# A fused attention and feed-forward kernel: the first output tiles prepared and projected inside the last attention group

## The chip, the cores and the metric

The kernel runs on one core of a Trainium2 chip. The metric is the device time of one execution in microseconds (us), the median of several runs. The engines are TensorE (PE; its weight loads are listed as PEld), VectorE (DVE), ScalarE (ACT), GpSimd (POOL) and SyncE (SP), which here only issues DMAs. Each engine works through its own program in order; they are tied together by semaphores.

## The reference

One layer on an input of 2 x 1024 x 512 in float32: attention with 32 heads of 16 numbers (queries and keys clipped and normalised, a linear position bias, a causal mask), an output projection, a residual, and then a normalised product with a weight summed from four sign matrices, with a residual again.

```python
    x = L0_attn_hidden_states
    x = x + _L0_attn_ref(_layernorm(x, axis=-1), L0_attn_Wqkv, ..., L0_attn_Wout)
    x = x + _L0_ffn_ref(_layernorm(x, axis=-1), L0_ffn_bases, L0_ffn_alphas)
    return x
```
Inside the attention `probs = softmax(scores)`, `out = einsum('bhqk,bkhd->bqhd', probs, v)` and the result is `einsum('bsd,ed->bse', out, Wout)`. Inside the second part `W_q = sum(alphas * bases, axis=0)` and the result is `einsum('bsi,oi->bso', x, W_q)`.

## The kernel before

The kernel has three stages in one program. Stage one projects 16 tiles of 128 tokens to queries, keys and values and stores them in device memory. Stage two is the attention. Stage three takes the 16 tiles again: the **output stage**.

**Attention.** There are 16 groups (0 to 15) of four heads; groups 0 to 7 are the first batch row, which is output tiles 0 to 7. A group has 12 units (a block of 128 keys against up to 512 queries), and the units are cut into 40 **entries** (`NE`), each one exponential on ACT (`probs<-ps`, L781). A step `s` of the loop `exp_step` is entry `s % 40` of group `s // 40`; the last group, 15, is steps 600 to 639, and its entries are called e0 to e39 below. At every step each engine emits what belongs to it. PE computes the scores of the entry in one of four rotating PSUM banks (L1098: a first product, and a second that is added to it; even entries use the lower 64 rows of the array and odd ones the upper 64), and six steps behind it multiplies a whole unit of exponentials with the values (L1133, called **weighing**). POOL masks the diagonal entries (L673), which are e0 to e11 and e28 to e39. Since there are four score banks, PE is at most four entries ahead of ACT. The running maxima of a group (PE L1078, DVE L951) are computed one group ahead, so that they are over before group 15 begins and DVE has nothing to do in it but the inversion below. When half a group is weighed, ACT copies it to `o_sb` (L809, `copy_half`) and SP stores it (L506). In group 15 the first copy comes at e18 and the second after e39.

**Output stage.** For each tile t, SP loads the attention output `o_in` and the reciprocal sums `inv_in` (L529, L532) and the residual `x2` (L536). POOL multiplies them (`att`, L687), ACT rounds the product to the short format (`att_hi`, L803), POOL takes the rest (`att_lo`, L691), and PE multiplies both with the output weight: 12 matmuls of 128x512, four each of L1012, L1013 and L1014, into PSUM bank 0 or 1. DVE adds the residual (L973), takes the statistics (L976, L978), ACT the square root (`y_sd`, L822), DVE the reciprocal and the normalised tile `yn` (L982, L986). PE transposes it (L1020, four matmuls), ACT and DVE split it into `yt_hi` and `yt_lo` (L829, L992), PE multiplies with the second weight (again 12 matmuls), DVE adds the residual (`y_out`, L1001) and SP stores the tile. The loop is staggered: in its step s PE does the projection of tile s+2, the transposes of s+1 and the second product of s.

**Weights.** Each of the two weights of this stage is kept as a rounded part and a rest. The rest `wffn_lo` of the second weight is made by POOL (`low_chunk`, L596, four chunks) after all steps of the attention. The tiles of the output stage share memory with the unrounded weights, so SP may load nothing into them before both weights are done (`wout_ready`, `wffn_ready`).

**Sums.** The sums of the exponentials of a batch row lie in device memory beside the attention output. SP loads them (`sums`, L542), DVE inverts them (`invert`, L956), SP stores the reciprocals (`inv_dram`, L547) and then loads them per tile in the wide form. For the first batch row this is done around group 15, for the second in the output stage.

The order on each engine is fixed by the program text: there is no scheduler. The parts of SP's program that matter are the function `group_step(s)` for s = 14 and 15, of which the second runs after SP has stored the halves of the groups before.

## Time and profile before

| | |
|---|---|
| runs | 725.4, 720.21, 721.72 us |
| median | 721.72 us |
| profiled execution | 724.78 us |
| its span in the profile | 723.0 us |
| busy: PE, DVE, ACT, POOL | 678.8, 575.2, 411.4, 312.9 us |
| mean granted TensorE clock | 0.962 |
| attention's last weighing ends | 609.84 us |
| last instruction (`y_out` of tile 15) starts | 719.82 us |

All times in the rows are microseconds from the start of the span. The 1.8 us between the span and the time of the profiled execution lie around the program.

### The profile page before, as it was taken

The page shows a single profiled execution, that of the slowest core. Times are in us where ns is not written, and L with a number is a line of the kernel's source. Part 1 is how long each engine was busy: PE and PEld are TensorE (multiplying, and loading weights), DVE is VectorE, ACT ScalarE, POOL GpSimd, SP SyncE. Part 2 cuts the span into 40 slices and gives each one's busy share as a digit, 9 for nine tenths or more (in the row PEclk, how much of TensorE's full clock was granted, in tenths as well). Part 3 has the DMA queues.
Part 4 walks back from the last instruction along what each step waited for, and adds up shares of the span by engine and source line. Part 5 has one row for each costly group of instructions (what it writes and reads, how often), then busy time and mean ns, then how long its engine had stood idle before and what let it go on. Part 6 is the DMA issues. An engine that isn't in the chain of part 4 may idle for free.

```text
span 723.0 us, 16007 instructions
## 1 busy us (share of the span) xinstructions
PE 678.8 (94%) x6096; PEld 416.4 (58%) x6096; DVE 575.2 (80%) x990; ACT 411.4 (57%) x855; POOL 312.9 (43%) x403
## 2 busy tenths in 40 slices
PE   3999999997999999999999999999899896599998
PEld 2888888883354454444455455444445532488886
DVE  6799999988999889998998899799899810275664
ACT  5132333232078778887787788678778886222221
POOL 1377777777034625525426422322332234444440
PEclk9999999997579999999999999999999999699999
DMA  8225556777884342343344334324434111635441
GB/s 297 65 68 174 175 175 194 199 201 215 264 183 106 117 127 86 98 125 116 90 123 122 91 108 125 110 78 125 114 94 117 50 35 23 170 103 156 145 148 66
DMA packets 102060, 93.64 MB, mean 130 GB/s; under 512 B 11640, under 2 KB 81912, under 8 KB 101984
## 3 DMA queue, kind: packets, MB, share of 16 engines
q1 hardware_dynamic: 97856, 86.84, 41.4%
q10 hardware_dynamic: 2016, 3.67, 1.7%
q0 software_dynamic: 2112, 2.10, 1.5%
q8 instruction: 49, 0.80, 0.5%
q14 instruction: 27, 0.22, 0.1%
HBM read 57.44 MB, written 33.82 MB: 126 GB/s over the span
## 4 chain that ended last, share of the span: by engine, by line
PE 71%; DVE 15%; issue 8%; POOL 3%; ACT 2%; DMA 1%; SPq 0%; DVEq 0%; POOLq 0%; ACTq 0%
PE ps L1098 23%; PE ps L1133 20%; PE ps L1078 9%; PE ps L1012 5%; PE ps L1013 5%; PE ps L1014 5%; DVE stats L951 3%; DVE qk_stat L896 2%; DVE qk L892 2%; PE ps L1020 2%; PE ps L1074 2%; DVE x_stat L862 1%; DVE xt_lo L855 1%; DVE rest L871 1%; DVE v_ext L905 1%
## 5 line engine op out<-in xcount | busy, mean ns | idle before, releaser
L951 DVE TENSOR_REDUCE stats<-ps 128x1 f32<-128x512 f32 (+3 forms) x608 | 359.4, 656 | 43.9 <-PE ps L1078 42.2
L781 ACT ACTIVATE probs<-ps 128x512 f32<-128x512 f32 (+2 forms) x640 | 310.2, 560 | 83.4 <-PE ps L1098 82.9
L1078 PE MATMUL ps<-first_k,first_q 54*128 54x128 bf16 (+3 forms) x1152 | 219.9, 284 | 5.6 <-DVE stats L951 5.2
L1098 PE MATMUL ps<-second_q,second_k 64*128 64x128 bf16 (+4 forms) x1152 | 206.2, 276 | 0.0
L1098 PE MATMUL ps<-first_q,first_k 54*128 54x512 bf16 (+3 forms) x768 | 197.0, 331 | 9.3 <-issue 9.2
L673 POOL TENSOR_SCALAR_AFFINE_SELECT probs<-probs 128x256 f32<-128x256 f32 x256 | 102.5, 406 | 144.2 <-ACT probs L781 136.9
L1133 PE MATMUL ps<-probs,v_sb 128*32 128x512 f32 (+3 forms) x1536 | 157.9, 498 | 1.8 <-issue 0.8
L1098 PEld LDWEIGHTS ps<-first_q,first_k 54*128 54x128 bf16 x768 | 58.2, 95 | 121.8 <-ACT probs L781 108.1
L1078 PEld LDWEIGHTS ps<-first_k,first_q 54*128 54x128 bf16 x1152 | 92.7, 96 | 49.3 <-DVE stats L951 34.7
L1098 PEld LDWEIGHTS ps<-second_q,second_k 50*128 50x128 bf16 (+1 forms) x1152 | 92.9, 96 | 21.4 <-issue 2.1
L1012 PE MATMUL ps<-wqkv_hi,xt_hi 128*128 128x512 f32 x192 | 77.3, 403 | 0.0
L1014 PE MATMUL ps<-wqkv_hi,xt_lo 128*128 128x512 f32 x192 | 75.8, 395 | 0.0
L1013 PE MATMUL ps<-wqkv_lo,xt_hi 128*128 128x512 f32 x192 | 75.7, 394 | 0.0
L614 POOL TENSOR_TENSOR qk<-qk,qk_gain 128x1024 f32<-128x1024 f32 x16 | 38.4, 2399 | 59.9 <-DVE qk L913 59.9
L653 POOL TENSOR_TENSOR shift_lo<-shift,shift_hi 32x128 bf16<-32x128 f32 x16 | 6.7, 418 | 131.8 <-ACT shift_hi L765 131.8
L973 DVE TENSOR_TENSOR x<-ps,x 128x512 f32<-128x512 f32 x16 | 11.0, 687 | 58.9 <-PE ps L1014 58.9
L1133 PEld LDWEIGHTS ps<-probs,v_sb 128*32 128x32 f32 x1536 | 33.9, 108 | 34.9 <-ACT probs L781 15.1
L1074 PE MATMUL ps<-mask_sb 64*128 64x256 bf16 x256 | 51.0, 280 | 0.0
L751 ACT ACTIVATE qk_sd<-qk_mv,eps 128x2 f32<-128x2 f32 x16 | 4.7, 296 | 69.6 <-DVE qk_mv L899 69.6
L1014 PEld LDWEIGHTS ps<-wqkv_hi,xt_lo 128*128 128x128 f32 x192 | 36.6, 191 | 8.0
L1012 PEld LDWEIGHTS ps<-wqkv_hi,xt_hi 128*128 128x128 f32 x192 | 36.8, 191 | 7.2
L1013 PEld LDWEIGHTS ps<-wqkv_lo,xt_hi 128*128 128x128 f32 x192 | 36.7, 191 | 7.2
(79 smaller groups left out, 822.1 us busy)
## 6 DMA issues: line engine op xcount, KB each, us to landing
parts_dram<-parts SPq DMA_DIRECT2D x48, 256.0 KB, 4.0
v_dram<-v_ext SPq DMA_DIRECT2D x16, 512.0 KB, 4.0
v_sb<-v_dram SPq DMA_DIRECT2D x16, 512.0 KB, 4.4
o_dram<-o_sb SPq DMA_DIRECT2D x32, 256.0 KB
first_q<-parts_dram SPq DMA_DIRECT2D x96, 64.0 KB
first_k<-parts_dram SPq DMA_DIRECT2D x96, 64.0 KB
second_q<-parts_dram SPq DMA_DIRECT2D x96, 64.0 KB
second_k<-parts_dram SPq DMA_DIRECT2D x96, 64.0 KB
```

Of the source, the lines that this page charges most:

```text
L614: pool.tensor_tensor(qk[t % 2][:], qk[t % 2][:], qk_gain[:], ALU.mult).then_inc(qk_scaled, 1)
L673: pool.affine_select(out=turned, in_=turned, compare_op=ALU.is_ge, fill=0.0, base=0, pattern=[[0, 2], [1, P]], channel_multiplier=-1).then ...
L781: act.activation(weights, scores, ACT.Exp, scale=SCALE).then_inc(exp_done, 1)
L892: dve.tensor_scalar(qk[t % 2][:], ps[:, bank:bank + 2, :], CLIP, -CLIP, ALU.min, ALU.max).then_inc(qk_clipped, 1)
L951: dve.tensor_reduce(to, scores, AX.X, ALU.max).then_inc(max_taken, 1)
L1012: pe.matmul(to, hi[:, c, :], w_hi[:, c, :], start=(c == 0), stop=False)
L1013: pe.matmul(to, hi[:, c, :], w_lo[:, c, :], start=False, stop=False)
L1014: last = pe.matmul(to, lo[:, c, :], w_hi[:, c, :], start=False, stop=(c == DC - 1))
L1074: pe.matmul(ps[:, bank, :].rearrange("p (r h t) -> p r h t", r=G, h=2)[:, :, h, :], late_q[h][mine, :], one_hot[mine, :, :], start=(h == 0 ...
L1078: last = pe.matmul(ps[:, bank, r * cols:(r + 1) * cols], first_q[n % STACKS][rows, hp, i * P:(i + 1) * P], first_k[n % STACKS][rows, hp, k ...
L1098: return pe.matmul(ps[:, bank, r * cols + first:r * cols + last], stack_k[n % STACKS][rows, heads[r] // PAIR, kb * P:(kb + 1) * P], stack_ ...
L1133: last = pe.matmul(ps[j * VW:(j + 1) * VW, PV_BANK, to:to + cols], v_sb[n % 2][:, kb, j * VW:(j + 1) * VW], probs[w % P_SLOTS][:, j, 0:col ...
```

## The change

Four things move from the output stage into groups 14 and 15.

- The four chunks of `wffn_lo` are made on POOL in the steps of group 14 (`LOW_AT`, entries 13, 16, 19 and 22).
- SP waits for both weights at the end of `group_step(14)`, then loads the sums, the three first residuals, stores the reciprocals and loads tiles 0 and 1; after the first `att` it loads tile 2. All of this now stands ahead of the stores of group 14's second half and of both halves of group 15. `load_sums` waits for the first batch row's stores alone.
- POOL multiplies tiles 0, 1 and 2 at e13, e15 and e22 of group 15 (`attend`), and takes the rests of tiles 0 and 1 at e18 and e20 (`low_attention`). ACT rounds them at e17, e19 and e30 (`high_attention`).
- PE projects tiles 0 and 1 in eight pieces of three matmuls, one behind each of the entries e24 to e31 (`PROJ_AT`). Tile 2 is projected after the last weighing, ahead of the transposes of tile 0. PE's wait for the last copy to `o_sb` is dropped.

```diff
+LOW_AT = [(GROUPS - 2) * NE + 13 + 3 * c for c in range(DC)]
+LAST_GROUP = (GROUPS - 1) * NE
+AHEAD = 2
+ATT_AT = [LAST_GROUP + 13, LAST_GROUP + 15, LAST_GROUP + 22]
+ATT_HIGH_AT = [LAST_GROUP + 17, LAST_GROUP + 19, LAST_GROUP + 30]
+ATT_LOW_AT = [LAST_GROUP + 18, LAST_GROUP + 20]
+PROJ_AT = [LAST_GROUP + 24 + c for c in range(AHEAD * DC)]
...
                 if s == GROUPS - 2:
-                    load_sums(0)
-                if s == GROUPS - 1:
-                    store_inverses(0)
-
-                    sp.wait_ge(inv_stored, 16)
+
                     sp.wait_ge(wout_ready, DC)
                     sp.wait_ge(wffn_ready, DC)
+                    load_sums(0)
                     for t in range(3):
-                        if t == 2:
-                            sp.wait_ge(att_ready, 1)
+                        load_residual(t)
+                    store_inverses(0)
+                    sp.wait_ge(inv_stored, 16)
+                    for t in range(AHEAD):
                         load_sums_of_tile(t)
-                        load_residual(t)
+                    sp.wait_ge(att_ready, 1)
+                    load_sums_of_tile(AHEAD)
...
-                    sp.wait_ge(o_stored[half], 16 * (GROUPS if b else GROUPS - 1 - half))
+                    sp.wait_ge(o_stored[half], 16 * GPB * (b + 1))
...
+                    if s == LOW_AT[c]:
+                        low_chunk(wffn_lo, wffn_sum, wffn_hi, wffn_hi_ready, wffn_ready, c)
+                if s in ATT_AT:
+                    attend(ATT_AT.index(s))
+                if s in ATT_LOW_AT:
+                    low_attention(ATT_LOW_AT.index(s))
...
             run_steps(pool, exp_step)
-            for c in range(DC):
-                low_chunk(wffn_lo, wffn_sum, wffn_hi, wffn_hi_ready, wffn_ready, c)
...
-                if s == GROUPS * NE:
-                    high_attention(0)
...
+                if s in ATT_HIGH_AT:
+                    high_attention(ATT_HIGH_AT.index(s))
+
                 e = s - PV_AFTER - COPY_AFTER
...
-                if s == (GROUPS - 1) * NE:
+                if s == LAST_GROUP - EARLY + 1:
                     invert(0)
...
+                if s in PROJ_AT:
+                    t, c = PROJ_AT.index(s) // DC, PROJ_AT.index(s) % DC
+                    if c == 0:
+                        pe.wait_ge(max_taken, NTAKE * GROUPS)
+                    project(t, c, c + 1)
...
-            pe.wait_ge(o_ready, 2 * GROUPS)
-
...
+                if s == -1:
+                    project(AHEAD)
+                elif AHEAD < t < TILES:
+                    project(t)
```

`attend(t)` and `low_attention(t)` hold the two POOL instructions that stood in `output_step`, with their waits; `project(t, first, end)` holds the matmuls of a projection for the chunks first to end, with its waits, and raises `proj_done` behind the last chunk. DVE's program has the same instructions in the same order as before.

PE's program in group 15, entries e24 and e25 (two products each) and the weighing behind them, before:

```order
L1098 MATMUL ps<-first_q,first_k 128x512 [waits exp_done]
L1098 MATMUL ps<-second_q,second_k 128x512
L1098 MATMUL ps<-first_q,first_k 128x512 [waits exp_done]
L1098 MATMUL ps<-second_q,second_k 128x512
L1133 MATMUL ps<-probs,v_sb 32x512 [waits exp_done]
L1133 MATMUL ps<-probs,v_sb 32x512 x3
```

and in the changed program, where L1034 to L1036 are the matmuls of a projection:

```order
L1120 MATMUL ps<-first_q,first_k 128x512 [waits exp_done]
L1120 MATMUL ps<-second_q,second_k 128x512
L1034 MATMUL ps<-wout_hi,att_hi 128x512 [waits att_lo_ready,wout_ready,max_taken]
L1035 MATMUL ps<-wout_lo,att_hi 128x512
L1036 MATMUL ps<-wout_hi,att_lo 128x512
L1120 MATMUL ps<-first_q,first_k 128x512 [waits exp_done]
L1120 MATMUL ps<-second_q,second_k 128x512
L1034 MATMUL ps<-wout_hi,att_hi 128x512
L1035 MATMUL ps<-wout_lo,att_hi 128x512
L1036 MATMUL ps<-wout_hi,att_lo 128x512
L1155 MATMUL ps<-probs,v_sb 32x512 [waits exp_done]
L1155 MATMUL ps<-probs,v_sb 32x512 x3
```

Two entries that followed each other directly now have three full-array matmuls between them; this pattern goes on for eight entries.

SP's program from the sums of the first batch row on (`x_0` is the residual tile), before:

```order
L542 DMA sums<-o_dram 128x256 [waits o_stored1,o_stored0]
L506 DMA o_dram<-o_sb 4x32x512 [waits o_ready] x2
L547 DMA inv_dram<-inv 128x256 [waits inverted]
L529 DMA o_in<-o_dram 128x4x128 [waits wffn_ready,wout_ready,inv_stored]
L532 DMA inv_in<-inv_dram 128x1x128
L536 DMA x_0<-in_x 128x512
L529 DMA o_in<-o_dram 128x4x128
L532 DMA inv_in<-inv_dram 128x1x128
L536 DMA x_1<-in_x 128x512
L529 DMA o_in<-o_dram 128x4x128 [waits att_ready]
```

and in the changed program:

```order
L551 DMA sums<-o_dram 128x256 [waits o_stored0,o_stored1,wffn_ready,wout_ready]
L545 DMA x_0<-in_x 128x512
L545 DMA x_1<-in_x 128x512
L545 DMA x_2<-in_x 128x512
L556 DMA inv_dram<-inv 128x256 [waits inverted]
L538 DMA o_in<-o_dram 128x4x128 [waits inv_stored]
L541 DMA inv_in<-inv_dram 128x1x128
L538 DMA o_in<-o_dram 128x4x128
L541 DMA inv_in<-inv_dram 128x1x128
L538 DMA o_in<-o_dram 128x4x128 [waits att_ready]
L541 DMA inv_in<-inv_dram 128x1x128
L515 DMA o_dram<-o_sb 4x32x512 [waits o_ready] x3
```

The two stores that stood between the sums and the reciprocals now come, with the last one, behind the three loads of tiles.

## Rows read from the trace of the kernel before

**Rows 1.** Windows: length, busy us of each engine (count), PEclk, DMA share, GB/s

```profile
609.30:631.00 21.70, 9.35 (x38) 6.95 (x39) 3.69 (x8) 3.84 (x6) 12.94 (x11) 0.69 0.47 126
631.00:720.00 89.00, 88.78 (x420) 73.03 (x418) 55.60 (x106) 20.45 (x44) 33.70 (x26) 1.00 0.41 126
...
612.00:613.00 1.00, 0.00 (x0) 0.00 (x0) 0.00 (x0) 0.00 (x0) 1.00 (x2) 0.65 0.00 0
```

**Rows 2.** Chain of waits that ended last, 609 to 631 us: start, us, what

```profile
609.27 4.91 POOL wffn_lo L596 x4
...
614.67 3.27 DMA inv_in<-inv_dram
618.01 1.27 POOL att L687
...
631.09 0.23 PE ps L1013
```

**Rows 3.** Timeline of SP, 584 to 629 us: start, us, engine, line, DMA

```profile
584.45 0.51 SPq L542 DMA_DIRECT2D sums<-o_dram  x1
...
620.80 0.55 SPq L506 DMA_DIRECT2D o_dram<-o_sb  x1
...
628.26 0.32 SPq L542 DMA_DIRECT2D sums<-o_dram  x1
```

**Rows 4.** Issue to landing of L542 (sums, two loads), then L547 (reciprocals, two stores)

```profile
DMA to landing us min/median/max: 2.0/2.1/2.2
...
DMA to landing us min/median/max: 2.3/3.9/5.5
```

**Rows 5.** Timeline of POOL: start, us, form, [idle before, releaser]

```profile
581.43 0.42 POOL L653 TENSOR_TENSOR shift_lo<-shift,shift_hi 32x128 bf16<-32x128 f32 x1 [11.00 <-ACT shift_hi L765]
```

**Rows 6.** Timeline of ACT in group 15 and at the stage's start

```profile
594.58 2.56 ACT L781 ACTIVATE probs<-ps 128x512 f32<-128x512 f32 x5 [0.20 <-PE ps L1098]
596.98 0.65 ACT L809 ACTIVATE o_sb<-ps 128x512 f32<-128x512 f32 x1
...
623.29 1.28 ACT L822 ACT_TABLE_LOAD   x1
...
628.34 0.29 ACT L822 ACTIVATE y_sd<-y_mv,eps 128x1 f32<-128x1 f32 x1 [3.77 <-DVE y_mv L978]
```

**Rows 7.** Timeline of PE in group 15

```profile
597.68 1.06 PE L1133 MATMUL ps<-probs,v_sb 128*32 128x512 f32 x8 [0.38 <-ACT o_sb L809]
...
599.12 0.41 PE L1098 MATMUL ps<-first_q,first_k 54*128 54x512 bf16 x2
...
599.68 1.06 PE L1133 MATMUL ps<-probs,v_sb 128*32 128x512 f32 x8
...
601.98 0.39 PE L1098 MATMUL ps<-first_q,first_k 54*128 54x512 bf16 x1
...
602.52 1.06 PE L1133 MATMUL ps<-probs,v_sb 128*32 128x512 f32 x8
...
603.97 0.33 PE L1098 MATMUL ps<-first_q,first_k 54*128 54x384 bf16 x2
...
609.42 0.42 PE L1133 MATMUL ps<-probs,v_sb 128*32 128x128 f32 x8 [0.17 <-POOL probs L673]
621.42 0.76 PE L1012 MATMUL ps<-wout_hi,att_hi 128*128 128x512 f32 x1 [11.58 <-POOL att_lo L691]
```

**Rows 8.** Timeline of DVE at the start of the output stage

```profile
626.56 0.69 DVE L973 TENSOR_TENSOR x<-ps,x 128x512 f32<-128x512 f32 x1 [38.17 <-PE ps L1014]
...
632.09 0.68 DVE L992 TENSOR_TENSOR yt_lo<-ps,yt_hi 128x512 fp32r<-128x512 f32 x1
632.69 1.74 DVE L956 RECIPROCAL inv<-sums 128x256 f32<-128x256 f32 x1
```

**Rows 9.** Timeline of PE there: first transposes, second product of tile 1

```profile
629.47 0.66 PE L1020 MATMUL ps<-ident,yn 128*128 128x128 f32 x4 [0.19 <-DVE yn L986]
...
639.73 0.47 PE L1012 MATMUL ps<-wffn_hi,yt_hi 128*128 128x512 f32 x1
```

More of the change, by code:

```diff
@@ L674, in exp_step, with attend, low_attention @@
                                            pattern=[[0, 2], [1, P]], channel_multiplier=-1).then_inc(masked, 1)
+            def attend(t):
+                pool.wait_ge(o_loaded[t % 2], 2 * 16 * (t // 2 + 1))
+                if t >= 2:
+                    pool.wait_ge(att_lo_ready, t - 1)
+                pool.tensor_tensor(att[t % 2][:], o_in[t % 2][:],
+                                   inv_in[t % 2][:].rearrange("p (a t) -> p a t", a=1).broadcast_to([P, DC, P]),
+                                   ALU.mult).then_inc(att_ready, 1)
+            def low_attention(t):
+                pool.wait_ge(att_hi_ready, t + 1)
+                pool.tensor_tensor(att_lo[t % 2][:], att[t % 2][:], att_hi[t % 2][:].bitcast(F32),
+                                   ALU.subtract).then_inc(att_lo_ready, 1)
             run_steps(pool, exp_step)
[L677 to L678 removed]
             def output_step(s):
                 t = s + 3
[L683 to L692 removed]
+                if AHEAD < t < TILES:
+                    attend(t)
+                if AHEAD <= t < TILES:
+                    low_attention(t)
             run_outputs(pool, output_step)
@@ L815, in output_step @@
                 t = s + 3
-                if 1 <= t < TILES:
+                if AHEAD < t < TILES:
                     high_attention(t)
@@ L1008, in _, with product @@
         def _(pe):
-            def product(to, hi, lo, w_hi, w_lo):
-                for c in range(DC):
+            def product(to, hi, lo, w_hi, w_lo, first=0, end=DC):
+                for c in range(first, end):
                     pe.matmul(to, hi[:, c, :], w_hi[:, c, :], start=(c == 0), stop=False)
@@ L1167, in exp_step, with project @@
                         weigh(e // NE * NU + u)
+            def project(t, first=0, end=DC):
+                if first == 0:
+                    if t == 0:
+                        pe.wait_ge(wout_ready, DC)
+                    pe.wait_ge(att_lo_ready, t + 1)
+                    if t >= 2:
+                        pe.wait_ge(x2_ready, t - 1)
+                last = product(ps[:, O_BANK[t % 2], :], att_hi[t % 2], att_lo[t % 2], wout_hi, wout_lo, first, end)
+                if end == DC:
+                    last.then_inc(proj_done, 1)
             run_tiles(pe, tile_step, -1, TILES - 1)
```

24 lines of the change are left out of this document (3 added, 21 removed).

## The prediction, made before the change was run

> **What bounds the kernel now.** I read the windows first. Between the attention and the full speed of the output stage lies a stretch of 21.7 us, 609.3 to 631, in which PE is busy 9.35 us, DVE 3.69 and ACT 3.84; behind it PE is busy 88.78 of 89 us [rows 1]. So there are two different limits: a chain of small steps up to 631, and PE's own work from there. PE's last weighing ends at 609.42 + 0.42 = 609.84, and its next matmul starts 11.58 us later, released by `att_lo` [rows 7]. The chain of waits names what lies between: 4.91 us of `wffn_lo` on POOL, 3.27 us until `inv_in` has landed, then `att` with 1.27 [rows 2], the rounding, and `att_lo`, which works on as many numbers as `att` on the same engine. Meanwhile PE's granted clock falls: 0.65 in 612 to 613, some 2.5 us after PE stopped, and 0.69 over the whole stretch, which mixes the full 2.4 GHz with 1.2 GHz [rows 1].
>
> In group 15 itself PE and ACT are in balance. PE takes e24 to e31 between 599.12 and 603.97, 4.85 us for eight entries and two weighings of about 1.0 us each (the rows say 1.06, with some overlap) [rows 7]; ACT needs 2.56 us for five exponentials, 0.51 each [rows 6], so 4.1 us for eight. There is no large hole in PE to fill.
>
> **The part that is removed.** I time the new stage from E, the end of the last weighing, and look for the start of the second product of tile 1, since from there PE is never idle again in either program. Before, that product starts at 639.73 [rows 9], which is E + 29.9.
>
> After the change, the four weight chunks (4.91 us) lie in group 14, where POOL idles 11.0 us in one piece before 581.43 [rows 5]: cost nothing. Loads and `att` of tiles 0 to 2 lie before E. Tile 2's projection waits for its `att_lo`, which POOL takes behind the last mask: 1.3 us, so it starts at about E + 0.8 and ends, with twelve matmuls of 0.23 us [rows 2], at E + 3.6. PE's gap of 0.8 us is too short for the fall of the clock, which came 2.5 us after the stop.
>
> Beside it runs tile 0's chain. ACT copies the last half (0.6 us), loads the table for the root (1.28) and takes the root [rows 6]: it begins at E + 0.2 + 0.6 + 1.3 = E + 2.1. Before, from this root (628.34) to the end of `yt_lo` of tile 0 (632.09 + 0.68 = 632.77) it took 4.43 us [rows 6, 8], with the same instructions on ACT and DVE in between. So the first second product starts at E + 6.6, and PE stands still for about 2.0 us before it, with the transposes of tile 1 at its end.
>
> Then DVE meets the inversion for the second batch row. Its sums can be loaded only when the last half is stored. Before, that store was issued at 620.80 and the load at 628.26, 7.5 us later, but behind the nine loads of tiles 0 to 2 that SP's program has just ahead of it; without them I take 5.5 us, the longer of the two landings of a store of reciprocals, 2.3 and 5.5 [rows 3, 4]. The store goes out at E + 0.9, the sums load at E + 6.4 and land 2.1 later [rows 4], and DVE inverts for 1.74 [rows 8]: E + 10.3. From there it is 2.91 us to the transposes of tile 2, as from 626.56 to 629.47 for tile 0 [rows 8, 9], and 0.5 more to the second product of tile 1: E + 13.8. PE's own work up to that point (project tile 3, transposes) would end at E + 12.7, so DVE's inversion is what comes last, by 1.1 us.
>
> The load of tile 3 is issued behind the last store, at E + 1.4; with 3.8 us from issue to `att` (the 3.27 of the chain and about 0.5 for issuing the load ahead of it) [rows 2, 3], 0 to 2 for the store ahead of it, and 3.3 for `att`, rounding and rest, its projection is ready at E + 8.5 to 10.5; PE arrives at E + 9.4, so even the late end only brings PE's own work to E + 13.8.
>
> Removed: 29.9 - 13.8 = **16.1 us**. Bounds: with the store landing after 7.5 us it is 14.1, with 3.5 us PE's own 12.7 counts and it is 17.2.
>
> **The part that is added, all of it ahead of E.** Two projections are 24 matmuls of 0.23 us, 5.5 us, on an engine that was in balance. And they stand between entries. Where two entries follow directly, their matmuls overlap (rows of two in one start; e24 and e25 from 599.12 to the weighing at 599.68, 0.28 us each); the entry that stood alone took from 601.98 to 602.52, 0.54 us [rows 7]. Now all eight stand alone: 8 x (0.54 + 0.69) + 2 x 1.0 = 11.8 us for e24 to e31, against 4.85. That is 7.0 us more. I add 0.3 for a weight load that can't be brought forward at some of the borders: 7.3. The bounds: if alone entries cost nothing extra, and the waits for ACT of about 1 us in this stretch are absorbed, 5.5 - 0.9 = 4.6; if each of the eight borders costs another 0.2, 8.6.
>
> Here a rule of the Trainium skill speaks against the change. TensorEngine Tiling (Array Packing), under Key Properties, says that a change of the tiling mode drains the engine. The entries run in halves of the array's rows and the projections in all of it, so there are sixteen such changes more. The 0.54 against 0.28 us agree with it; without the rule the sum would be 5.5 - 0.9, with it the 7.3 above.
>
> ACT's rounding of tile 0 at e17 stands ahead of the copy of the first half, for which PE already waits at 597.68 (0.38 us idle) [rows 7]. So its 0.6 us moves PE: 0.6. The roundings at e19 and e30 fall where PE is the slower one: nothing.
>
> Whether `att` is there in time is the uncertain term. The sums' load at 584.45 lands as before, 2.2 us later at most, and DVE has inverted them 1.74 us later, at 588.4 [rows 3, 4, 8]. The reciprocals' store then queues behind the three residual loads that SP has just issued; with 2.3 to 5.5 us of landing [rows 4] it is there at 590.7 to 593.9. Tile 0's loads need the same 3.8 us from issue to `att`, `att` 1.27 [rows 2]: 595.8 to 599.0. ACT reaches the rounding when its exponential e17 is done, at about 596.6, 0.4 before the copy at 596.98 [rows 6]. POOL is free then, since it has no mask between e11 and e28. So the wait is 0 to 2.4 us. I take 0.2, nearer the lower end, since the queue ahead of the store holds only residual loads that were issued two to three us earlier. If it is late, ACT stops, PE stops four entries later, and behind them the copy, the weighing and everything else.
>
> SP now stands at its wait for the first `att` with three stores behind it. The store of group 14's second half goes out at about 597 instead of 591; who waits for it is only the last copy, at E. The store of the first half of group 15 goes out behind it at about 598, as before. Nothing is lost.
>
> Added: 7.3 + 0.6 + 0.2 = **8.1 us**, bounds 5.2 and 11.6.
>
> **The sum.** 16.1 - 8.1 = 8.0 us less: the span goes from 723.0 to 715.0 and the profiled execution from 724.8 to 716.8. That execution lies 3.1 us above the median of the three runs; applied to the median, 721.7 - 8.0 = **713.7 us**. No measurement of this kernel can tell less than about 1% from no change, 7.2 us.
>
> **Rivals.**
> - *The tiles come late.* The reciprocals' store takes 5.5 us and `att` of tile 0 ends at 599.0: 2.2 us more. For it: three transfers in a row (sums, reciprocals, tile), each with its landing, in 12 us. Against: the queue is nearly empty there. Time 715.9. Chance 0.17.
> - *The projections are cheap.* The drain is small and they fill waits: 4.6 instead of 7.3. For it: PE waits for ACT in this stretch. Against: the lone entry's 0.54. Time 711.0. Chance 0.15.
> - *The clock falls.* In the new start PE pauses 0.8 us, works 2.8, pauses 2.0, transposes, and pauses again. Before, the clock fell 2.5 us into a pause. The mean of 0.69 over 21.7 us means 13.5 us at the lower level, so it lasted from 612.3 to 625.8, the last 4.4 of it with PE at work from 621.42 [rows 1, 7]: 2.2 us lost. If it falls here as well, 2.2 us go back. Time 715.9. Against: no single pause reaches 2.5 us. Chance 0.12.
> - *It gets slower.* One mechanism: ACT's rounding at e17 waits for the three transfers, and with it all exponentials. Each us of lateness is a us of the end. It decides when tile 0's `att` ends after 596.8 + 8.0 = 604.8, that is when the landings of the reciprocals and of the tile take together 8 us longer than I took. With 10 us more it is 723.7. Only the saturated queue from 614 to 620 could do that, and it brought tile 0 in 3.27 us [rows 2]. Chance 0.03.
> - *It doesn't do what it says*: the masks or a semaphore keep the projections out of the attention, and they run after E with the rest. Then their 5.5 us fall behind E and nothing is paid in group 15 but 0.8: 16.1 - 5.5 - 0.8 = 9.8 less, 711.9. Chance 0.03.
>
> The forecast has 0.50. The range goes from 709.5 (cheap projections and a quick last store) to 718.5 (late tiles with expensive borders). Faster by over 1%, below 714.5: most of the forecast, all of the cheap case and the last one, 0.58. Within 1%: the rest of the forecast, late tiles, the clock, 0.38. Slower: 0.04.
>
> **What would show it.** In the new profile, right: no `wffn_lo` behind the last mask; PE's first projection matmul between entries; e24 to e31 taking 11 to 13 us on PE, ACT idle there with PE as releaser; from the last weighing to the second product of tile 1 about 14 us instead of 29.9, with DVE idle before the second inversion until the sums land; granted clock 1.00 throughout. Wrong: ACT idle for over 1 us before the rounding of tile 0 (late tiles); PE's stretch under 10 us (cheap borders); matmuls of 0.43 us behind E (clock); PE's steady stretch of 5.9 us per tile broken up by waits for `att_lo`, which would mean that SP's program is late behind the new stores and would hit every later tile.

## The result, and the profile after

The changed kernel takes 720.75 us (median of 20 runs, 714.92 to 727.81) where the kernel before takes 723.67 (20 runs beside them, 718.91 to 727.27). The ratio is 0.995, with an interval of 0.9927 to 0.9973: 3.6 us less, between 2.0 and 5.3. That is faster, by less than 1%, and outside the range that was forecast. The ratio is of the means of the runs in the fast state, which leaves out two of the changed kernel, 726.38 and 727.81 us; its other 18 lie between 714.92 and 724.64.

The profiled execution of the changed kernel took 715.26 us, with a span of 713.4. That is 9.6 us under the span before, but only about half of it is the change. I cut both traces at S, the issue of the first load of sums (584.45 before [rows 3], 579.69 after), behind which everything that the change does on the critical path lies. From S to the end of the span it is 138.55 us before and 133.71 after: **4.84 us less**, which lies inside the interval of the runs. The other 4.8 us lie ahead of S. I do not count them as the change's: in the kernels below that leave the program ahead of S as it is after the change, S comes anywhere from 579.18 to 587.32, and the last section shows what makes it move. I call the stretch from S to the end R, and compare profiles by it; E is, as in the prediction, the end of the last weighing.

The timeline of PE of the kernel after (start, us, line, tiles, count, idle before and releaser), group 15 and the start of the output stage. L1120 is the scores, L1155 the weighing, L1034 to L1036 the three matmuls of a product:

```profile
593.37 1.07 PE L1155 MATMUL ps<-probs,v_sb 128*32 128x512 f32 x8 [0.88 <-ACT o_sb L831]
...
594.87 0.39 PE L1120 MATMUL ps<-first_q,first_k 54*128 54x512 bf16 x1
...
598.72 0.39 PE L1120 MATMUL ps<-first_q,first_k 54*128 54x512 bf16 x1
598.94 0.38 PE L1120 MATMUL ps<-second_q,second_k 50*128 50x512 bf16 x1
599.25 0.50 PE L1034 MATMUL ps<-wout_hi,att_hi 128*128 128x512 f32 x1
599.59 0.39 PE L1035 MATMUL ps<-wout_lo,att_hi 128*128 128x512 f32 x1
599.82 0.40 PE L1036 MATMUL ps<-wout_hi,att_lo 128*128 128x512 f32 x1
600.15 0.39 PE L1120 MATMUL ps<-first_q,first_k 54*128 54x512 bf16 x1
...
608.30 0.34 PE L1120 MATMUL ps<-first_q,first_k 54*128 54x384 bf16 x2
...
613.62 0.43 PE L1155 MATMUL ps<-probs,v_sb 128*32 128x128 f32 x8 [0.17 <-POOL probs L688]
614.77 0.50 PE L1034 MATMUL ps<-wout_hi,att_hi 128*128 128x512 f32 x1 [0.72 <-POOL att_lo L703]
...
619.90 0.66 PE L1042 MATMUL ps<-ident,yn 128*128 128x128 f32 x4 [1.69 <-DVE yn L1008]
620.60 0.47 PE L1034 MATMUL ps<-wffn_hi,yt_hi 128*128 128x512 f32 x1
...
621.59 0.63 PE L1034 MATMUL ps<-wffn_hi,yt_hi 128*128 128x512 f32 x1
622.02 0.63 PE L1035 MATMUL ps<-wffn_lo,yt_hi 128*128 128x512 f32 x1
...
626.91 0.50 PE L1034 MATMUL ps<-wout_hi,att_hi 128*128 128x512 f32 x1 [1.74 <-POOL att_lo L703]
...
630.12 0.48 PE L1034 MATMUL ps<-wffn_hi,yt_hi 128*128 128x512 f32 x1
```

To be seen: E is 613.62 + 0.43 = 614.05. The pieces of the projections stand between the entries as planned. From e24 (594.87) to e32 (608.30) PE takes 13.43 us, against 4.85 [rows 7]. Behind E the first product starts at E + 0.72, where before PE stood still for 11.58 us. The second product of tile 0 starts at 620.60, E + 6.55; that of tile 1 at 630.12, E + 16.07, against E + 29.9 [rows 9]. From there to the end of the span both kernels take the same (83.28 us here, 83.27 before).

So 13.8 us went behind E, and from S to E the kernel became longer, 34.36 us instead of 25.39: 9.0 were added. 13.8 - 9.0 is the 4.8.

The chain of waits of the kernel after (start, us, what) tells what holds the second start up:

```profile
614.10 0.61 ACT o_sb L831
...
614.73 0.50 SPq L515
...
615.27 0.48 SPq L538
...
615.79 7.70 DMA inv_in<-inv_dram
...
623.56 1.28 POOL att L696
...
625.58 1.28 POOL att_lo L703
...
626.91 0.50 PE ps L1034
```

Tile 3's load needs 7.70 us to land, where the same row before said 3.27 [rows 2]. Beside it in the timeline of SP:

```profile
591.86 23.37 SPq L515 DMA_DIRECT2D o_dram<-o_sb  x3
...
622.00 0.34 SPq L551 DMA_DIRECT2D sums<-o_dram  x1
```

The last of the three stores (the chain puts it at 614.73) has landed when SP issues the sums' load at 622.00, after 7.27 us, with nothing queued in front of it. And the clock fell, in the windows of the kernel after (length, busy us and count of each engine, granted clock, DMA share, GB/s):

```profile
618.00:620.00 2.00, 0.31 (x3) 0.10 (x2) 1.46 (x5) 0.78 (x2) 0.00 (x0) 1.00 0.24 70
620.00:622.00 2.00, 1.97 (x8) 1.47 (x9) 0.45 (x1) 0.00 (x0) 0.00 (x0) 0.77 0.24 78
622.00:624.00 2.00, 2.00 (x6) 1.59 (x5) 0.00 (x0) 0.00 (x0) 0.44 (x1) 0.50 0.49 131
624.00:626.00 2.00, 1.17 (x4) 0.57 (x3) 1.93 (x2) 0.63 (x1) 1.26 (x2) 0.88 0.88 223
```

0.50 is the lower level, 1.2 GHz, and the matmuls of the first second product follow one another by 0.43 us (621.59, 622.02) instead of 0.23. The DMA share of 0.24 in 618 to 622 is the other thing to keep in mind: the store and the rest of tile 3's load were under way, and no more than a quarter of the sixteen engines' time was in use.

The trace also records the steps in which each DMA counts up the semaphore that reports its landing. A load of the sums counts up in sixteen steps close together (623.86 to 624.04). The last whole store has only five: one at 615.65, 0.9 us after its issue, and four at 620.38 to 621.93. Tile 3's two loads, `o_in` and `inv_in`, share a semaphore: after one early step it has twelve steps by 618.69, then none until 621.17, and eight from there to 623.50. So twelve steps were over 3.4 us after the first of the two was issued, and the other eight came only with the store's four and behind them.

### The profile page after: what moved, and what is told of

It reads as the page before. It is cut to its first block, busy times and chain, and to the rows that moved or that the text cites. A ratio compares the mean times of both kernels' runs of the same rounds, so it can differ in the third digit from the quotient of the medians.

```text
span 713.4 us, 16008 instructions
## 1 busy us (share of the span) xinstructions
PE 679.0 (95%) x6096; PEld 413.8 (58%) x6096; DVE 574.4 (81%) x990; ACT 412.0 (58%) x855; POOL 313.6 (44%) x403
## 4 chain that ended last, share of the span: by engine, by line
PE 72%; DVE 15%; issue 8%; DMA 2%; ACT 1%; POOL 1%; SPq 0%; DVEq 0%; POOLq 0%; ACTq 0%
PE ps L1120 23%; PE ps L1155 20%; PE ps L1100 9%; PE ps L1034 5%; PE ps L1035 5%; PE ps L1036 5%; DVE stats L973 3%; DVE qk_stat L918 2%; DVE qk L914 2%; PE ps L1042 2%; PE ps L1096 2%; DVE x_stat L884 1%; DVE xt_lo L877 1%; DMA inv_in<-inv_dram 1%; DVE rest L893 1%
## 5 line engine op out<-in xcount | busy, mean ns | idle before, releaser
L1120 PE MATMUL ps<-second_q,second_k 64*128 64x128 bf16 (+4 forms) x1152 | 205.9, 274 | 0.0
L1120 PE MATMUL ps<-first_q,first_k 54*128 54x512 bf16 (+3 forms) x768 | 196.5, 328 | 7.7 <-issue 7.7
L1155 PE MATMUL ps<-probs,v_sb 128*32 128x512 f32 (+3 forms) x1536 | 157.0, 496 | 2.1 <-ACT o_sb L831 1.2
L1120 PEld LDWEIGHTS ps<-first_q,first_k 54*128 54x128 bf16 x768 | 58.1, 94 | 121.2 <-ACT probs L800 107.6
L1120 PEld LDWEIGHTS ps<-second_q,second_k 50*128 50x128 bf16 (+1 forms) x1152 | 92.0, 95 | 20.1 <-issue 0.6
L1034 PE MATMUL ps<-wqkv_hi,xt_hi 128*128 128x512 f32 x192 | 77.1, 402 | 0.0
L1036 PE MATMUL ps<-wqkv_hi,xt_lo 128*128 128x512 f32 x192 | 75.6, 394 | 0.0
L1155 PEld LDWEIGHTS ps<-probs,v_sb 128*32 128x32 f32 x1536 | 33.8, 108 | 34.9 <-ACT probs L800 15.3
L1036 PEld LDWEIGHTS ps<-wqkv_hi,xt_lo 128*128 128x128 f32 x192 | 36.5, 190 | 8.0
L1034 PEld LDWEIGHTS ps<-wqkv_hi,xt_hi 128*128 128x128 f32 x192 | 36.6, 191 | 7.1
```

Of the source, the lines that this page charges most:

```text
L1034: pe.matmul(to, hi[:, c, :], w_hi[:, c, :], start=(c == 0), stop=False)
L1036: last = pe.matmul(to, lo[:, c, :], w_hi[:, c, :], start=False, stop=(c == DC - 1))
L1120: return pe.matmul(ps[:, bank, r * cols + first:r * cols + last], stack_k[n % STACKS][rows, heads[r] // PAIR, kb * P:(kb + 1) * P], stack_ ...
L1155: last = pe.matmul(ps[j * VW:(j + 1) * VW, PV_BANK, to:to + cols], v_sb[n % 2][:, kb, j * VW:(j + 1) * VW], probs[w % P_SLOTS][:, j, 0:col ...
```

## The experiments

They ask three things: what the projections between entries cost, what the late landings cost and why they are late, and which part of the change earns the gain. No kernel leaves work out. Their numbers, with S, E and R from the one profiled execution of each:

| kernel | median us (runs) | ratio to before, interval | S | E - S | second product of tile 1, from E | R |
|---|---|---|---|---|---|---|
| before | 723.67 (20) | | 584.45 | 25.39 | 29.89 | 138.55 |
| after | 720.75 (20) | 0.995 (0.9927 to 0.9973) | 579.69 | 34.36 | 16.07 | 133.71 |
| e1 | 709.95 (6) | 0.9817 (0.9783 to 0.9852) | 579.18 | 26.35 | 16.15 | 125.82 |
| e2 | 715.67 (4) | 0.9902 (0.9863 to 0.9941) | 580.95 | 34.35 | 14.08 | 132.05 |
| e3 | 702.45 (4) | 0.9718 (0.9683 to 0.9754) | 570.32 | 34.41 | 12.70 | 130.48 |
| e4 | 717.67 (10) | 0.9925 (0.9896 to 0.9953) | 587.32 | 32.54 | 17.49 | 133.38 |
| e5 | 714.28 (4) | 0.9875 (0.9829 to 0.9922) | 583.31 | 25.40 | 20.62 | 129.29 |
| e6 | 711.19 (6) | 0.9843 (0.9809 to 0.9877) | 570.57 | 25.46 | 29.54 | 138.33 |
| e7 | 698.33 (6) | 0.9667 (0.9633 to 0.97) | 570.63 | 26.42 | 16.16 | 125.87 |
| e9 | 697.63 (4) | 0.966 (0.9611 to 0.9708) | 570.05 | 26.42 | 15.66 | 125.35 |

Ratios are to the kernel before on the same chip; its median there was 723.19 for e1 to e4 and 721.89 for e5 to e9.

### e1: both projections behind the attention

```diff
-PROJ_AT = [LAST_GROUP + 24 + c for c in range(AHEAD * DC)]
+PROJ_AT = []
-ATT_HIGH_AT = [LAST_GROUP + 17, LAST_GROUP + 19, LAST_GROUP + 30]
+ATT_HIGH_AT = [LAST_GROUP + 17, LAST_GROUP + 19]
...
+            high_attention(AHEAD)
...
-                if s == -1:
-                    project(AHEAD)
-                elif AHEAD < t < TILES:
+                if 0 <= t < TILES:
                     project(t)
```

> The changed kernel, but with the projections of tiles 0 and 1 not in group 15: PE does them behind the last weighing, in the old order, and ACT rounds tile 2 there. Everything else (low weights in group 14, early loads, early products of tiles 0 to 2) stays. I read it by the stretch R from the issue of the sums' load at the end of group 14 to the end of the span: 138.55 us before the change, 133.71 after it. Theory A (the eight interleaved pieces cost 8.6 us on PE, and behind the last weighing PE would have had 5.5 us of room for them, since it stands waiting for tile 3): the last weighing comes 8.6 us earlier, PE is busy from it on without a pause over 1 us, and R is about 125; ratio to the kernel before about 0.981. Theory B (the pieces fill time in which PE waits for ACT anyway): the last weighing comes only 3 to 5 us earlier, R stays at 132 to 135, ratio about 0.993 to 0.997.

Measured: E - S falls from 34.36 to 26.35, by 8.0 us, and the second start does not move (16.15 after E instead of 16.07). Both are what theory A had said (8.6 us earlier, R about 125, no pause over 1 us). In PE's timeline of e1 nearly all of its idle time of the new start is gone:

```profile
611.64 0.66 PE L1043 MATMUL ps<-ident,yn 128*128 128x128 f32 x4 [0.45 <-DVE yn L1009]
...
618.47 0.50 PE L1035 MATMUL ps<-wout_hi,att_hi 128*128 128x512 f32 x1 [0.19 <-POOL att_lo L703]
```

What follows: the interleaved projections are pure cost. PE has 8.0 us too much to do ahead of E, and behind E it is waiting for transfers anyway, so the same 24 matmuls are free there. R is 7.9 shorter than after the change, and the ratio is 0.9817 instead of 0.995.

E - S is still 1.0 us above that of the kernel before. Counted from S, PE's weighings come as early as before until the one at 592.86, which waits for ACT's copy behind the rounding at e17 and is 0.45 us late. The next one, at 595.37, is 0.95 late: between them ACT has rounded tile 1 at e19.

```profile
593.13 0.68 ACT L825 ACTIVATE att_hi<-att 128x512 fp32r<-128x512 f32 x1
```

### e2: tile 3 loaded before the last store

```diff
                     sp.wait_ge(att_ready, 1)
                     load_sums_of_tile(AHEAD)
+                    sp.wait_ge(att_ready, 2)
+                    load_sums_of_tile(AHEAD + 1)
...
-                if 3 <= t < TILES:
+                if 4 <= t < TILES:
```

> The changed kernel with one reordering on SP: the load of tile 3 is issued as soon as POOL has multiplied tile 1, ahead of the last three stores of the attention output. Theory A (tile 3's load lands 7.7 us after its issue because it queues behind the last store, and this is the last thing PE waits for, with DVE's inversion 1.2 us behind it): the second product of tile 1 starts 1.0 to 1.3 us earlier, at E + 15.1 instead of E + 16.3 (E is the end of the last weighing), now released by DVE; R 132.5. Theory B (the load isn't what holds PE): no change, R 133.7. Theory C (only tile 3 was late): the second product of tile 1 starts at E + 12.7, R 130.1.

Measured: the projection of tile 3 starts at E + 10.97 instead of 12.86, the second product of tile 1 at E + 14.08 instead of 16.07, and R is 1.7 us shorter. That lies between theory A (E + 15.1) and theory C (E + 12.7): tile 3 was not the only thing that was late, but without its load the store lands earlier too. The sums' load goes out at E + 6.52 instead of 7.95. The timeline of SP of e2, and its windows behind the last store:

```profile
594.34 22.14 SPq L515 DMA_DIRECT2D o_dram<-o_sb  x3
621.82 0.33 SPq L553 DMA_DIRECT2D sums<-o_dram  x1
```

```profile
619.00:621.00 2.00, 0.47 (x5) 0.23 (x3) 1.46 (x4) 0.97 (x3) 0.00 (x0) 1.00 0.25 91
621.00:623.00 2.00, 1.81 (x7) 1.41 (x8) 0.70 (x2) 0.33 (x1) 1.27 (x1) 0.74 0.12 28
623.00:625.00 2.00, 2.00 (x6) 1.52 (x6) 1.13 (x1) 0.00 (x0) 0.00 (x0) 0.50 0.80 209
```

The last of the three stores is issued at about 594.34 + 22.14 - 0.5 = 616.0 and has landed at 621.8: 5.8 us when it is alone, against 7.27 with tile 3's load beside it. So each of the two transfers makes the other late. With tile 3 there in time, PE waits for nothing after the first second product; what is last in e2 is the lower clock, under which that product ran (from its start at 621.85 to the next projection at 626.27 it is 4.4 us, instead of 2.8). At the full clock PE would have been there 1.6 us earlier, but DVE's chain from the inversion at 623.87 would have kept the start at E + 13.4 to 13.8 (an estimate: 4.5 us from the start of the inversion to the end of `yn`, as from 624.07 in the kernel after, and 0.36 to 0.70 for the transposes, as at 629.76 and 619.90 there), so 0.3 to 0.7 of them count.

### e3: each store of outputs cut into four

The store writes a tile of 128 rows whose pattern in DRAM has a first dimension of 4. Here it is four stores of 32 rows each, with the same bytes (the counts of `o_stored` that ACT and SP wait for are four times as high):

```diff
-                        sp.dma_start(o_dram[n // GPB, :, ds((n % GPB) * G, G), half * BANK:(half + 1) * BANK]
-                                     .rearrange("r j t -> j r t"), o_sb[half][:]).then_inc(o_stored[half], 16)
+                        for j in range(G):
+                            sp.dma_start(o_dram[n // GPB, :, (n % GPB) * G + j, half * BANK:(half + 1) * BANK],
+                                         o_sb[half][j * VW:(j + 1) * VW, :]).then_inc(o_stored[half], 16)
```

> The changed kernel with every store of half a group's attention output cut into four stores of 32 rows, one per head, instead of one whose outermost dimension is 4. Theory A (the one store is worked on by 4 of the 16 DMA engines, which is why it takes 7.3 us to land with an otherwise empty queue and why tile 3's load, issued behind it, takes 7.7): in the trace the DMA share rises above 0.25 during the last store, it lands within 2 to 4 us of its issue, the second inversion begins 3 us earlier, tile 3 arrives 2 to 4 us earlier and the second product of tile 1 starts at E + 12.7 to 14; R 130.1 to 131.4. Theory B (the 7.3 us are fixed costs of a store to device memory): landing unchanged or later by the 1 us of three more issues, R 133.7 to 134.7.

Measured: 702.45 us, 0.9718. Behind E it does what it was made for, and theory A holds in every point. The timeline of SP of e3, and its windows behind the last store (E is 604.73):

```profile
582.29 24.83 SPq L516 DMA_DIRECT2D o_dram<-o_sb  x12
...
608.51 0.34 SPq L552 DMA_DIRECT2D sums<-o_dram  x1
```

```profile
606.00:608.00 2.00, 2.00 (x10) 1.65 (x9) 0.94 (x3) 0.98 (x2) 0.00 (x0) 1.00 0.54 131
608.00:610.00 2.00, 0.91 (x7) 0.54 (x5) 1.42 (x5) 0.54 (x2) 0.00 (x0) 1.00 0.65 178
```

The sums' load goes out at E + 3.78 instead of E + 7.95, and the share of the DMA engines is more than twice as high (0.54 to 0.65 against 0.24). The semaphore of tile 3's loads, which had the gap from 618.69 to 621.17 in the kernel after, here has all its steps but the early one between 609.51 and 610.78, without a gap. The second start comes at E + 12.70, which is PE's own work at the full clock: the prediction had worked out E + 12.7 for that case. The clock stays at 1.00, which is 0.3 to 0.7 us of the difference to e2's 14.08; the rest is the inversion, which begins at E + 7.11 instead of 8.57.

But that is 3.2 us of R, and the kernel is 18 us faster than after the change. The rest lies ahead of S, which comes at 570.32. The waits of PE by line, of the kernel before (us in total, times, longest):

```profile
PE ps L1098 <- issue: 9.2, 7, 1.9
```

and of e3, where the scores are on L1121 and that line no longer has a row of this kind:

```profile
PE ps L1101 <- DVE stats L974: 4.7, 3, 2.4
...
PE ps L1156 <- issue: 0.8, 2, 0.5
```

What stands in the way at these places are small loads from SBUF to SBUF, `second_q` from `shift_hi` and `shift_lo`, from issue to landing (us, least, median and most of 64), before:

```profile
DMA to landing us min/median/max: 1.7/2.7/5.0
```

and in e3:

```profile
DMA to landing us min/median/max: 1.7/1.8/3.3
```

The profile names no releaser for the seven waits ("issue"), but the times of the landings do. Six of them, of 0.83 to 1.91 us, each end 0.1 us after the last step with which the group's four small loads land; in the kernel after it is seven of sixteen groups, in e3 none. And the late steps come with a whole store. For the wait that ends at 252.66, 48 of the 64 steps of the four loads are over at 250.39; the other sixteen come at 251.48 to 252.56, right behind the four late steps of the whole store issued at 242.99 (251.30 to 251.82).

How often it happens differs from run to run: e3's runs lie between 702.40 and 702.63, those of the kernel after between 714.92 and 724.64.

### e4: pieces of six matmuls, four borders instead of eight

```diff
-PROJ_AT = [LAST_GROUP + 24 + c for c in range(AHEAD * DC)]
+PROJ_AT = [LAST_GROUP + 25 + 4 * c for c in range(AHEAD * 2)]
-                    t, c = PROJ_AT.index(s) // DC, PROJ_AT.index(s) % DC
+                    t, c = PROJ_AT.index(s) // 2, PROJ_AT.index(s) % 2 * 2
...
-                    project(t, c, c + 1)
+                    project(t, c, c + 2)
```

(and the rounding of tile 2 at e34 instead of e30.)

> The changed kernel with the two early projections in four pieces of six matmuls, at entries e25, e29, e33 and e37, directly ahead of a weighing, instead of eight pieces of three behind each of e24 to e31. Theory A (half of the price is the border: an entry between projections stands alone, 0.54 us instead of 0.28, and another 0.2 us go at each border): only four borders and no lone entries, the last weighing comes 2.2 to 3 us earlier, R 130.7 to 131.5. Theory B (the price is the 24 matmuls and the rounding on ACT alone, and the borders are free): R within 0.5 of 133.7. Theory C (blocks of six matmuls drain the four score banks and starve ACT, which then can't catch up): R above 134.5.

Measured: E - S is 32.54, 1.8 us less for four pairs of borders and the entries that they leave alone, with the same matmuls: 0.45 us for a pair. Theory A had 2.2 to 3; part of what is missing is that PE now waits for ACT again (0.25 us at 607.39). R is only 0.3 shorter, which is theory B's number, but not by its reason, since the last weighing did come earlier: the clock fell in a worse place. Windows of e4, whose projection of tile 3 starts at 632.79 after a pause of 3.41 us:

```profile
632.00:634.00 2.00, 1.21 (x3) 1.02 (x4) 1.90 (x3) 0.00 (x0) 1.97 (x2) 0.58 0.11 34
634.00:636.00 2.00, 2.00 (x7) 1.58 (x6) 1.53 (x5) 1.30 (x3) 0.33 (x1) 0.57 0.00 0
```

Between E and the second start it lost what it had won before E. For the price of a border the run counts; for the time of the kernel (0.9925, whose interval overlaps that of the change) it is inconclusive.

### e5: the kernel before, with the low weights in group 14 and nothing else

```diff
+LOW_AT = [(GROUPS - 2) * NE + 13 + 3 * c for c in range(DC)]
...
+                    if s == LOW_AT[c]:
+                        low_chunk(wffn_lo, wffn_sum, wffn_hi, wffn_hi_ready, wffn_ready, c)
...
-            for c in range(DC):
-                low_chunk(wffn_lo, wffn_sum, wffn_hi, wffn_hi_ready, wffn_ready, c)
```

> The kernel before with one part of the change alone: the four chunks of the second weight's rest are made on POOL in group 14. Nothing else moves. R is the stretch from the issue of the first batch row's sums' load (end of group 14) to the end of the span, 138.55 us before, 133.71 in the changed kernel. Theory A (the chain behind the attention is a sum of its steps, and this part's 4.91 us come off it whole): PE's first projection starts 6.7 us behind the last weighing instead of 11.6, R is 133.3 to 134.1, ratio about 0.993, which is all that the whole change brings. Theory B (another wait stands behind it, the reciprocals' store or the loads): R 135 to 138.5.

Measured: 714.28 us, 0.9875; R is 9.3 us shorter than before, more than either theory gave. PE's pause behind E is 2.81 us instead of 11.58. That is 8.77 = 4.91 for the chunks + 3.86 more. (The remaining 0.5 us of the 9.3 is the clock: PE's first product behind E ran at 0.43 us a matmul for 3.5 us, before for 4.5.) The reason is in the waits of SP's queue. Before:

```profile
SPq L520 <- POOL wffn_lo L596: 15.4, 1, 15.4
```

In SP's program the wait for all chunks of weights stands ahead of the loads of tile 0. In e5 that row is gone, and the timeline of SP has the loads, whose landing took 3.27 us behind the chunks [rows 2], before E (608.71):

```profile
602.67 0.38 SPq L530 DMA_DIRECT2D o_in<-o_dram  x1
```

So this one part, four lines, is worth about twice the whole change. All the other parts together take another 4.5 us from the tail (20.62 to 16.07) and cost 9.0 ahead of E.

### e6: the kernel before, with stores cut

The edit of e3 on the kernel before, with its counts.

> The kernel before, with every store of half a group's attention output cut into four stores of 32 rows, and no part of the change. Theory A (the store on few DMA engines also holds up the small loads of the row maxima that SP issues behind it in every group, for which PE waits at the start of a group, 9.2 us in seven waits; it has nothing to do with the change): these waits are gone, the sums' load of group 14 is issued near 575 us instead of 584, R stays at 138 to 139, the runs lie within 1 us of each other, ratio 0.985 to 0.989. Theory B (the 9 us that the changed kernel gained ahead of group 15 from this edit come from its own new order of SP's work): ratio above 0.995.

Measured: 711.19 us, 0.9843, runs from 710.09 to 711.56. R is 138.33, as before the change (138.55), and S comes at 570.57. The waits of PE for the scores are gone, as theory A had it; the rest came out a little beside its numbers (575 for S, runs within 1 us of each other, 0.985 to 0.989). What follows: the gain ahead of S, 14 us in this pair of profiles and 11 us by the medians, has nothing to do with the change. Of the 14 us, 9.2 are those waits, and about 3.4 the clock, which in the kernel before was at 0.50 for 3.4 us behind each of two of them (from 253.91 and from 458.71; half of that time is lost).

### e7 and e9: everything that helped

e7 is e1, e2 and e3 together; e9 is e1 and e3.

> The changed kernel with three edits together: projections of tiles 0 and 1 behind the last weighing, tile 3's load ahead of the last stores, and every store of the attention output cut into four. Theory A (the three causes are separate): from the last weighing on PE has no pause over 0.5 us, the second product of tile 1 starts at E + 15.5 to 15.8, R is 125.0 to 125.6, the stretch ahead of it as with the cut stores alone, so the span is 695.5 to 696.5 us and the ratio to the kernel before 0.964 to 0.966. Theory B (with the stores cut, the tail of the changed kernel with its early projections is short enough, 96.1 us behind E, that taking the projections back costs 3 of the 8 us): that is contained in A; a ratio above 0.969 would say that something else has become late.

> The same without the early load of tile 3. Theory A (with the stores cut, the load of tile 3 behind the last store comes in time, since PE has two more projections to do first): same as the run with it within 0.3 us, R 125.0 to 125.9. Theory B (the early load is still needed): R 0.5 to 1.5 us longer.

Measured: 698.33 and 697.63 us, 0.9667 and 0.966. The fastest version is the change without the interleaving and with cut stores, 24 us below the kernel before. The early load of tile 3 adds nothing once the stores land quickly: e9's R is 125.35, e7's 125.87, which is 0.3 above the range given for e7, and the second product of tile 1 came at E + 16.16 where 15.5 to 15.8 was expected. Of PE's pauses behind E one is left, in the timeline of e9:

```profile
602.58 0.66 PE L1044 MATMUL ps<-ident,yn 128*128 128x128 f32 x4 [0.45 <-DVE yn L1010]
```

e7 shows 0.96 in its place: DVE's `yn` of tile 0 took 1.05 us there (from 602.56) instead of 0.55, while POOL was at work on an `att` (from 602.05); in e9 POOL's next `att` waits for its tile and starts only at 602.85, behind `yn`. Whether the one slowed the other no run here shows.

No run puts e5 and e6 together. From e5's R (129.29), e6's S (570.57) and the 1.8 us around the span, an estimate for that kernel is 701.7 us, so of the 24 us about 20 would come from these two small edits and 4 from the rest of the change.

## Why the prediction was wrong

The direction and the order of things were right, the size was not: -8.0 forecast, -4.8 in the profiles, -3.6 (2.0 to 5.3) by the runs. The failed step is the sum's first term, the time behind E, which was too high by 2.3; the term ahead of E was too low by 0.9. Of the 7 us between 713.7 and the measured 720.75, 2.0 are neither: the sum started from 721.72, the median of three runs, and 20 runs have 723.67. And with 20 runs of each kernel the interval is 0.23% to either side, where I had put the limit of what can be told at 1%.

**Behind E: 16.1 forecast, 13.8 measured.** Up to E + 6.6 every step held: first product at E + 0.72 (0.8), first second product at E + 6.55 (6.6). The failure is in one sentence: "without them I take 5.5 us" for the last store. It took 7.27. For the store by itself 5.5 was nearly right (5.8 in e2), though by luck: I had taken it from stores of reciprocals, which are of another size and pattern. But tile 3's load is issued 0.5 us behind the store, and I priced each as if the other were done or gone. With the load beside it the store took 1.4 us more, and the load, for which I took "3.8 ... 0 to 2 for the store ahead of it", 7.70 from its last issue to landing, so that its projection came at E + 12.86 rather than 8.5 to 10.5, and it, not DVE's inversion (begun at E + 10.02, forecast end 10.3, real end 11.8), came last. By DVE's chain from the inversion alone the second start would have come at E + 14.9 to 15.2 (an estimate, worked out as for e2), so the late inversion is 1.1 to 1.4 of the 2.3 us and the late tile 3 the rest. The load was late for a reason that I had not looked for at all: store and load were both served in part by a few of the DMA engines, as the steps of their landing show. e2 takes this load away and gets 14.08, with the clock down; e3 makes both transfers quick and gets 12.70, PE's own end as I had worked it out. The bound of 14.1 that I gave for a landing of 7.5 moved DVE's chain alone and left tile 3's load where it was; that is why it did not hold the 13.8.

**Ahead of E: 8.1 forecast, 9.0 measured.** The projections cost 13.43 - 4.85 = 8.6, not 7.3: the row of the upper bound, "if each of the eight borders costs another 0.2". One piece with its entry is 600.15 - 598.72 = 1.43 us: 0.53 for the entry and the change of kind, then 0.34, 0.23 and 0.33 for the three matmuls, where I had 0.54 + 0.69. So the first matmul behind the border and the last ahead of the next entry each take 0.1 more. e4 agrees in size, with 0.45 us for a pair of borders and its lone entries. By e1, which takes them out, they cost 8.0 in all, since E - S there is 1.0 above before. ACT's rounding at e17 made PE wait 0.88 instead of 0.38, so 0.5 where I took 0.6. The other half is its rounding at e19, for which I took nothing, "where PE is the slower one": in e1 it moves PE by 0.5; in the kernel after it is hidden behind the projections. `att` of tile 0 was not late (0.2 taken): ACT rounds it at 591.69 without a wait. The reciprocals' store was there in under 2 us, which is the empty queue that I had argued for.

The rule cited in the prediction, of the Trainium skill's TensorEngine Tiling (Array Packing), Key Properties, that a change of mode drains the engine, agrees with this trace: 1.43 us for a piece against 0.28 + 0.69 without borders. But it explains at most part of the 0.46 us between them. 0.26 are 0.54 - 0.28, what an entry loses when it no longer overlaps with its neighbour, and that needs no drain; about 0.2 are left for the two borders, and no run separates a drain from other causes there.

**The clock.** "No single pause reaches 2.5 us" did not keep it up: it fell behind pauses of 0.72 and 1.69 us. In the kernel after it cost PE about 1.6 us and the end nothing, since PE then waited 1.74 us for tile 3 all the same. As a rival it had 0.12 and was priced at 2.2, which is the right order: in e2 and e4, where nothing hides it, it costs the end 0.3 to 0.7 and 1.4 us (14.08 against DVE's chain, which I put at 13.4 to 13.8 there; 17.49 against 16.07).

**What I did not weigh.** PE is the bound ahead of E and waits for transfers behind it. I had both facts, and still asked only what the interleaving costs, not what the same 24 matmuls would cost behind E: by e1, 0.1 us. The rival "it doesn't do what it says", where the projections run after E, is e1 by another name: I charged it 5.5 us there and still had it at 711.9, below my forecast. It measured 709.95, with both projections covered by the wait for the last store. Nor did I see that the chunks of weights hold up SP's loads as well, so that moving them alone would bring 8.8 us of the 11.6.

## What to carry to other kernels

Before work is moved ahead of a bound, look at what the engine will be doing in the place from which it is taken: if it waits there for a transfer, the work is free where it stands. Of a wait that a change removes, ask first which single statement holds it up; here four moved instructions were worth twice the whole rebuild. And price a transfer by its own kind: a store that works on a quarter of the DMA engines is slow by itself, and makes small loads late that share no data with it.

## What the runs showed that I had not expected

**A store with a first dimension of 4 works on a quarter of the DMA engines.** The share is 0.25 where it is alone (619 to 621 in e2), its semaphore counts up in one early and four late steps where the load of the sums has sixteen, and it took 5.8 us from issue to landing, 7.27 with tile 3's load beside it. Cut into four, the last of its parts has landed 3.78 us after E, some 3.1 us after the copy of the outputs was done. On the way the small loads land in a median of 1.8 us instead of 2.7, and the kernel before becomes 0.9843 of its time. That the small loads wait on the same engines as the stores is my reading of this. The trace names no engine; what it shows is that they get quicker when the stores are cut, and that in the case at 252.66 sixteen of the 64 steps of four loads, as many as four of sixteen engines would make, come late and just behind the store's own four.

The Trainium skill has the rule for it, in DMA: Bandwidth & Descriptors, the section on why a DMA increments its semaphore by 16: the number of engines is the largest up to 16 that divides the slowest dimension of both patterns. For 4 that is 4 of 16, and the share of 0.25 agrees. Which engines are taken no run here shows.

One more DMA of this kind is left in every kernel here: `inv_in`, whose source is read with a first dimension of 4 (the 32 rows of reciprocals repeated for each quarter of the partitions). A tile's two loads make 21 steps, sixteen and five. In the kernel after, the last steps of tile 3's loads came at 622.66 to 623.50. No run changes this load.

**The spread of the runs was not noise.** It was 10 us wide for the kernel after and 0.2 us for e3, and over all kernels 3.4 to 10 us with whole stores (4 to 20 runs each) and 0.2 to 1.5 with cut ones (4 to 6 runs each). S in the four kernels with cut stores lies within 0.6 us (570.05 to 570.63), in the others within 8.1. For those six profiles the waits of PE for the scores, and half of the time that the clock then spent at 0.50 ahead of S, account for nearly all of that:

| | S | waits for the scores | half the time at 0.50 | what is left |
|---|---|---|---|---|
| before | 584.45 | 9.2 | 3.4 | 571.8 |
| after | 579.69 | 7.7 | 0 | 572.0 |
| e1 | 579.18 | 7.8 | 0 | 571.4 |
| e2 | 580.95 | 7.5 | 1.7 | 571.8 |
| e4 | 587.32 | 11.4 | 5.1 | 570.8 |
| e5 | 583.31 | 8.5 | 3.4 | 571.4 |

So a kernel that spreads more than its neighbours can have a race between transfers and engines that is worth looking for.

**The clock does not follow one pause.** Behind the same two pauses, 0.72 and 1.67 to 1.69 us, it was 0.50 in the next product in the kernel after and in e2, and 1.00 in e3 and e4, whose PE does the same work up to there. In e4 it fell only behind the pause of 3.41. In e1, where PE's pauses in that stretch are 0.45 and 0.19 us, it stays at 1.00. In the attention of the kernel before it fell behind waits of 1.71 and 1.68 us (until 252.66 and 457.72), and not behind waits of 1.69 and 1.91 (until 330.35 and 510.87). What decides between them no run here shows, so a plan for this stage has to reckon with either.
